# Quantised MLP of a small transformer stack: steps beside the roundings moved to GpSimd, scale chains in two parts, end tiles by halves

## The reference

```
def act_qdq(x):                                   # 16 bits, one scale for the whole tensor
    scale = max(max(abs(x)) / 32767, 1e-12)
    return clip(round(x / scale), -32768, 32767) * scale
def fixed_qdq_u16(x):
    return clip(round(x * 65536), 0, 65535) / 65536
x    = act_qdq(layernorm(x))
up   = act_qdq(x @ Wup.T)                         # Wup, Wgate, Wdown rounded to 4 bits in blocks of 32
gate = act_qdq(x @ Wgate.T)
sig  = fixed_qdq_u16(sigmoid(gate))
gate = act_qdq(gate * sig)
o    = act_qdq(gate * up)
out  = x0 + o @ Wdown.T
```

## Time and profile before

| what | value |
|---|---|
| time, median of 3 runs | 1922.03 us (1918.44 to 1930.69) |
| the profiled execution's own time | 1920.83 us |
| its span in the profile | 1919.0 us |
| mean granted TensorE clock | 0.96 of full speed |
| busy: TensorE, VectorE, ScalarE, GpSimd | 92%, 75%, 61%, 19% of the span |
| the quantised MLP in the profile | from about 1792 us to the end |

### The profile page before, as it was taken

One profiled execution on the slowest core, in us unless ns is written; L12 is line 12 of the kernel. 1 busy time (PEld: TensorE's weight loads), 2 busy tenths in 40 slices (PEclk: granted clock), 3 DMA queues, 4 the chain that ended last, 5 costly groups with the idle time before them and its releaser, 6 DMA issues. The chain is left out here.

```text
span 1919.0 us, 32646 instructions
## 1 busy us (share of the span) xinstructions
PE 1757.6 (92%) x12516; PEld 1206.2 (63%) x12516; DVE 1447.0 (75%) x1661; ACT 1173.2 (61%) x2107; POOL 369.9 (19%) x244
## 2 busy tenths in 40 slices
PE   6988989989999997999988899999999999999855
PEld 5877877457757775878776455555555555555524
DVE  6546643577899884565664799999999999997575
ACT  0333332577777764353531588888888888887373
POOL 4133120144445532232312000010010000000000
PEclk8999999999999998999989899999999999999887
DMA  9698780248866861122226855656666465540000
GB/s 358 256 350 326 273 301 1 93 161 294 319 236 243 312 237 46 68 72 69 72 36 112 170 94 123 120 100 111 118 114 115 95 120 107 104 73 8 1 0 22
DMA packets 171814, 279.78 MB, mean 146 GB/s; under 512 B 21854, under 2 KB 100478, under 8 KB 164494
## 3 DMA queue, kind: packets, MB, share of 16 engines
q1 hardware_dynamic: 170366, 277.52, 51.5%
q10 hardware_dynamic: 1296, 0.19, 0.1%
HBM read 187.07 MB, written 88.14 MB: 143 GB/s over the span
## 5 line engine op out<-in xcount | busy, mean ns | idle before, releaser
L2406 DVE TENSOR_REDUCE xn_peaks<-psum 128x2 f32<-128x1024 f32 x512 | 621.9, 1224 | 46.6 <-PE psum L2204 38.5
L2361 ACT ACTIVATE moe_mix_transposed<-psum 128x512 f32<-128x512 f32 x1024 | 552.9, 597 | 71.2 <-PE psum L2209 38.4
L2209 PE MATMUL psum<-xn_q_stack,xn_k_words 50*128 50x256 f32 x2048 | 377.3, 306 | 12.5 <-ACT y_normed L2331 5.6
L2209 PEld LDWEIGHTS psum<-xn_q_stack,xn_k_words 50*128 50x128 f32 x2048 | 249.7, 186 | 213.2 <-ACT moe_mix_transposed L2361 184.9
L2204 PE MATMUL psum<-xn_k_words,xn_q_stack 50*128 50x512 f32 x1024 | 373.3, 452 | 6.0 <-DMA xn_q_stack<-q_rows 3.8
L2241 PE MATMUL psum<-moe_mix_transposed,xn_v 128*32 128x256 f32 x4096 | 328.5, 392 | 1.9 <-issue 0.3
L2204 PEld LDWEIGHTS psum<-xn_k_words,xn_q_stack 50*128 50x128 f32 x1024 | 185.7, 185 | 14.2 <-DVE xn_peaks L2406 7.8
L934 POOL TENSOR_TENSOR mx_state<-mx_du,mx_b_all_channels 128x1024 f32<-128x1024 f32 x64 | 154.3, 2411 | 194.4 <-ACT mx_b_all_channels L1116 82.7
L1197 DVE TENSOR_TENSOR_SCAN mx_state<-psum,mx_state 128x1024 f32<-128x1024 f32 x64 | 146.2, 2285 | 49.4 <-ACT psum L1126 41.8
L324 PE MATMUL psum<-xw_ctx_natural,xw_weights_transposed 128*128 128x256 f32 x512 | 125.9, 392 | 13.5 <-DVE xw_weights_transposed L476 13.2
L2241 PEld LDWEIGHTS psum<-moe_mix_transposed,xn_v 128*32 128x32 f32 x4096 | 81.8, 108 | 74.4 <-issue 8.3
(11 more groups left out here) (351 smaller groups left out, 2549.6 us busy)
## 6 DMA issues: line engine op xcount, KB each, us to landing
xn_k_words<-k_words SPq DMA_DIRECT2D x384, 128.0 KB, 6.6
ctx_words<-xw_ctx_transposed_words SPq DMA_DIRECT2D x64, 512.0 KB
ctx_chunk_words<-ctx_words SPq DMA_DIRECT2D x64, 512.0 KB, 5.4
k_words<-ctx_k_words SPq DMA_DIRECT2D x128, 256.0 KB, 2.5
v_all<-ctx_v SPq DMA_DIRECT2D x32, 544.0 KB, 3.2
xn_v<-v_all SPq DMA_DIRECT2D x32, 544.0 KB, 4.8
xw_mask<-in_mask_BxSxS_ik SPq DMA_DIRECT2D x8, 2048.0 KB, 7.9
xw_ctx_natural<-in_ctx SPq DMA_DIRECT2D x32, 512.0 KB, 6.8
```

Of the source, the lines that this page charges most:

```text
L2209: return pe.matmul(PS[:, narrow_bank("exp", n, step, a), half * S:(half + 1) * S], K[n % XN_KSLOTS][narrow_rows(a), kt * P:(kt + 1) * P], ...
L2361: act.activation(t["weights"][:, step % 4, a, :, :], bank.rearrange("p (t s) -> p t s", t=2), ACT.Exp, scale=XN_SCALE).then_inc(s.taken, 1)
L2406: dve.tensor_reduce(t["peaks"][:, m % 2, q, :, c], PS[:, 2 * (x % 2):2 * (x % 2) + 2, :], AX.X, ALU.max).then_inc(s.top_read, 1)
```

## The change

GpSimd gets a function of its own, `mlp_pool`. It takes three kinds of steps: the subtraction of the rounding constant from the gate tiles 1 to 5 and from all up tiles (before: VectorE), the scaling and adding of the constant for the sigmoid (before: ScalarE), and the subtraction and clipping of the sigmoid (before: VectorE). In the first loop its order is gate tile m + 1, then the two sigmoid steps of tile m; VectorE keeps gate tile 0.

`scale_of` is cut in two: `spread_of` has the steps up to the diagonal, `scale_of` those behind the matmul. For scale 2 the first part now stands ahead of the last gate-times-sigmoid product and the second part right behind it.

End tiles go by halves: the gate projection of tile 0 waits for the first half of the rounded y only; the peak of the last gate tile is taken in two halves; tile 0 of the last product is rounded on VectorE, both steps, in two halves of 512 tokens, and the down projections of the first four token tiles wait for the first half only.

```diff
 def mlp_pe
     def projected(call, m, wT, made):
         for half in range(ML_HALVES):
+            if call == 0:
+                pe.wait_ge(s.q_y, KD * (half + 1))
...
-        pe.wait_ge(s.q_y, 2 * KD)
...
-        pe.wait_ge(s.q_out, m + 1)
+        pe.wait_ge(s.q_out, m + 2 if m else i * ML_HALVES // NT + 1)
...
 def mlp_act
         act.activation(t["sig"][:, m, :], t["gate"][:, m, :], ACT.Sigmoid, scale=t["scales"][:, 1, 0:1]).then_inc(s.sg, 1)
-        act.wait_ge(s.sg, m + 1)
-        act.activation(t["sig"][:, m, :], t["sig"][:, m, :], ACT.Identity, bias=k.round[:, 0:1],
-                       scale=ML_U_STEPS).then_inc(s.sr, 1)
...
-    for m in range(ML_IT):
+    for m in range(1, ML_IT):
         rounded(t["gate"][:, m, :], t["gate"][:, m, :], 4, s.r_out)
...
+def mlp_pool(k, t, s):
+    pool = k.pool
+    def gate_whole(m):
+        pool.wait_ge(s.r_gate, m + 1)
+        pool.tensor_scalar(t["gate"][:, m, :], t["gate"][:, m, :], FFN_ROUND, None, ALU.subtract).then_inc(s.q_gate, 1)
+    def sigmoid_steps(m):
+        sig = t["sig"][:, m, :]
+        pool.wait_ge(s.sg, m + 1)
+        pool.tensor_scalar(sig, sig, ML_U_STEPS, FFN_ROUND, ALU.mult, ALU.add).then_inc(s.sr, 1)
+        pool.wait_ge(s.sr, m + 1)
+        pool.tensor_scalar(sig, sig, FFN_ROUND, ML_U_STEPS - 1.0, ALU.subtract, ALU.min).then_inc(s.sq, 1)
+    pool.wait_ge(s.q_gate, 1)
+    gate_whole(1)
+    sigmoid_steps(0)
+    for m in range(1, ML_IT):
+        if m + 1 < ML_IT:
+            gate_whole(m + 1)
+        sigmoid_steps(m)
     for m in range(ML_IT):
+        pool.wait_ge(s.r_up, m + 1)
+        pool.tensor_scalar(t["up"][:, m, :], t["up"][:, m, :], FFN_ROUND, None, ALU.subtract).then_inc(s.q_up, 1)
...
 def mlp_dve
+    for half in range(ML_HALVES):
+        dve.wait_ge(s.gate, 2 * (ML_IT - 1) + half + 1)
+        largest(1, ML_IT - 1 + half, t["gate"][:, ML_IT - 1, half * BANK:(half + 1) * BANK], s.peak_gate)
...
     for m in range(ML_IT):
-        if m == 0:
-            up_largest(0)
-        if m + 1 < ML_IT:
-            gate_whole(m + 1)
-        if m:
-            up_largest(m)
-        dve.wait_ge(s.sr, m + 1)
-        dve.tensor_scalar(t["sig"][:, m, :], t["sig"][:, m, :], FFN_ROUND, ML_U_STEPS - 1.0, ALU.subtract,
-                          ALU.min).then_inc(s.sq, 1)
+        up_largest(m)
+        if m == ML_IT - 1:
+            spread_of(2, ML_IT, s.peak_up)
+        dve.wait_ge(s.q_gate, m + 1)
         dve.wait_ge(s.sq, m + 1)
         dve.scalar_tensor_tensor(t["gate"][:, m, :], t["sig"][:, m, :], 1.0 / ML_U_STEPS, t["gate"][:, m, :], ALU.mult,
                                  ALU.mult).then_inc(s.gated, 1)
+        if m == ML_IT - 1:
+            scale_of(2)
         dve.wait_ge(s.gated, m + 1)
         largest(3, m, t["gate"][:, m, :], s.peak_act)
-    scale_of(2, ML_IT, s.peak_up)
+    spread_of(3, ML_IT, s.peak_act)
     dve.wait_ge(s.unit, 2)
-    scale_of(3, ML_IT, s.peak_act, gated)
+    scale_of(3, gated)
...
     for m in range(ML_IT):
-        whole(t["up"][:, m, :], s.r_up, m, s.q_up)
         dve.wait_ge(s.r_act, m + 1)
         dve.wait_ge(s.q_up, m + 1)
...
+    spread_of(4, ML_IT, s.peak_out)
+    scale_of(4, product)
+    dve.wait_ge(s.scale, 5)
+    for half in range(ML_HALVES):
+        v = t["gate"][:, 0, half * BANK:(half + 1) * BANK]
+        dve.tensor_scalar(v, v, scales[:, 4, 1:2], FFN_ROUND, ALU.mult, ALU.add).then_inc(s.raised, 1)
+        dve.wait_ge(s.raised, half + 1)
+        dve.tensor_scalar(v, v, FFN_ROUND, None, ALU.subtract).then_inc(s.q_out, 1)
+    for m in range(1, ML_IT):
+        whole(t["gate"][:, m, :], s.r_out, m - 1, s.q_out)
```

More of the change, by code:

```diff
@@ L2918, in mlp_tiles @@
     return {"upT": k.ffn_upT, "gateT": k.ffn_gateT, "downT": k.ffn_downT,
-            "peak": sb("peak", [P, 5, ML_IT]), "top": sb("top", [P, 5]),
+            "peak": sb("peak", [P, 5, ML_IT + 1]), "top": sb("top", [P, 5]),
             "diagonal": sb("diagonal", [P, P]), "most": sb("most", [P, 5]), "unit": sb("unit", [P, 3, 2]),
@@ L2928, in mlp_sems @@
                         "most_pe most step inverse scale unit r_y q_y r_gate q_gate r_up q_up r_act r_out q_out sg sr sq gated "
-                        "product out x")
+                        "product raised out x")
 def mlp_pe(k, t, s):
@@ L3043, in mlp_act @@
         rounded(t["gate"][:, m, :], t["gate"][:, m, :], 3, s.r_act)
+    for m in range(1, ML_IT):
+        rounded(t["gate"][:, m, :], t["gate"][:, m, :], 4, s.r_out)
+def mlp_pool(k, t, s):
[16 more added lines that the diff above has]
+        sigmoid_steps(m)
     for m in range(ML_IT):
-        rounded(t["gate"][:, m, :], t["gate"][:, m, :], 4, s.r_out)
+        pool.wait_ge(s.r_up, m + 1)
+        pool.tensor_scalar(t["up"][:, m, :], t["up"][:, m, :], FFN_ROUND, None, ALU.subtract).then_inc(s.q_up, 1)
 def mlp_dve(k, t, s):
@@ L3053, in largest, with spread_of @@
         dve.tensor_reduce(peak[:, n, m:m + 1], v, AX.X, ALU.max, apply_absolute_value=True).then_inc(there, 1)
-    def scale_of(n, parts, there, of=None):
+    def spread_of(n, parts, there):
         dve.wait_ge(there, parts)
@@ L3062, in scale_of @@
         dve.tensor_scalar(t["diagonal"][:], k.ident[:], t["top"][:, n:n + 1], None, ALU.mult).then_inc(s.diagonal, 1)
+    def scale_of(n, of=None):
         dve.wait_ge(s.most_pe, n + 1)
@@ L3088, in whole @@
         dve.tensor_scalar(v, v, FFN_ROUND, None, ALU.subtract).then_inc(there, 1)
-    def gate_whole(m):
-        whole(t["gate"][:, m, :], s.r_gate, m, s.q_gate)
     def up_largest(m):
@@ L3100, in mlp_dve @@
         largest(0, g, k.Y[:, 4 * g:4 * (g + 1), :].rearrange("p t d -> p (t d)"), s.peak_y)
-    scale_of(0, KD, s.peak_y)
+    spread_of(0, KD, s.peak_y)
+    scale_of(0)
     for g in range(NT // 4):
@@ L3104, in mlp_dve @@
             whole(k.YT[:, c, g * BANK:(g + 1) * BANK], s.r_y, KD * g + c, s.q_y)
-    for m in range(ML_IT):
+    for m in range(ML_IT - 1):
         dve.wait_ge(s.gate, 2 * m + 2)
         largest(1, m, t["gate"][:, m, :], s.peak_gate)
-    scale_of(1, ML_IT, s.peak_gate)
+    for half in range(ML_HALVES):
+        dve.wait_ge(s.gate, 2 * (ML_IT - 1) + half + 1)
+        largest(1, ML_IT - 1 + half, t["gate"][:, ML_IT - 1, half * BANK:(half + 1) * BANK], s.peak_gate)
+    spread_of(1, ML_IT + 1, s.peak_gate)
+    scale_of(1)
     gated = unit_of(0, 1)
-    gate_whole(0)
+    whole(t["gate"][:, 0, :], s.r_gate, 0, s.q_gate)
     for m in range(ML_IT):
-        if m == 0:
-            up_largest(0)
-        if m + 1 < ML_IT:
-            gate_whole(m + 1)
-        if m:
-            up_largest(m)
-        dve.wait_ge(s.sr, m + 1)
-        dve.tensor_scalar(t["sig"][:, m, :], t["sig"][:, m, :], FFN_ROUND, ML_U_STEPS - 1.0, ALU.subtract,
-                          ALU.min).then_inc(s.sq, 1)
+        up_largest(m)
+        if m == ML_IT - 1:
+            spread_of(2, ML_IT, s.peak_up)
+        dve.wait_ge(s.q_gate, m + 1)
         dve.wait_ge(s.sq, m + 1)
@@ L3139, in mlp_dve @@
     dve.wait_ge(s.unit, 4)
-    scale_of(4, ML_IT, s.peak_out, product)
-    for m in range(ML_IT):
-        whole(t["gate"][:, m, :], s.r_out, m, s.q_out)
+    spread_of(4, ML_IT, s.peak_out)
[8 more added lines that the diff above has]
+        whole(t["gate"][:, m, :], s.r_out, m - 1, s.q_out)
     dve.wait_ge(s.scale, 5)
@@ L3152, in quantised_mlp @@
         t, s = mlp_tiles(k, scope), mlp_sems(k)
-        for engine in (mlp_pe, mlp_act, mlp_dve):
+        for engine in (mlp_pe, mlp_act, mlp_pool, mlp_dve):
             engine(k, t, s)
```

## The result

| | before | changed |
|---|---|---|
| median of the runs | 1922.03 us (7 runs, 1918.44 to 1936.03) | 1941.94 us (7 runs, 1927.18 to 1945.09) |
| ratio to before, 95% interval | | 1.0079 (1.0053 to 1.0106), 10 to 20 us slower |
| profiled execution | 1920.83 us, span 1919.0 | 1942.2 us, span 1940.4 |
| last block: start of the last variance step to the end of the span | 126.4 us | 138.8 us |

The kernel got slower, as forecast, but by less: 1942 us instead of 1953, and by the ratio's 0.8%, some 15 us, instead of the 31 forecast. (The ratio is the recorded estimate over all runs; the quotient of the two medians is 1.0104.)

The account below looks back on a forecast made before the run. VectorE's queue was taken as the path, with GpSimd becoming every product's supplier. Loop 1 +26.4 (start gain inside), scales +1.6, loop 2 +3.8, end -1.1 gave +30.7 us: 1953 us, 1.6% slower, range 1914 to 1966.

Parts of the forecast that it names:

- start to scale 1: Gate projections: TensorE may begin after two of four rounded pieces of y instead of four, gaining 1.3 us.
- loop 1: Loop over gate, sigmoid and up: GpSimd's queue of 17 steps delays the last product; cost 26.4 us, start gain inside.
- last product to scale 3: Scales 2 and 3: chain 3's diagonal meets GpSimd's first up step and waits to 4.8 us; cost 1.6 us.
- loop 2: Product loop: five GpSimd steps with four waits make it 23.5 us instead of 19.7; cost 3.8 us.
- end: Before the down projections: VectorE rounds half a tile in both steps, so TensorE starts earlier; gain 1.1 us.
- the exclusion of 1.0 us a turn: Both loops: VectorE products and GpSimd steps exclude each other; GpSimd waits about 1.0 us behind each product, bounds 0 and 1.23.
- T = 2.9 us: Estimated time of every moved GpSimd tensor_scalar on 128x1024 f32, extrapolated from smaller rows; bounds 2.4 and 3.3 us.
- steps under 2 us and two-operation steps far from one-operation ones: GpSimd step times in the new profile that the prediction said would make it wrong.
- The mechanism: Loop over gate, sigmoid and up: GpSimd, with 17 steps in one queue, 3 a turn, becomes the supplier of every product.
- The line-rate rival: GpSimd runs the moved steps at the cast's slope, 1.3 us each: -6 us, 1916 us; chance 0.18.
- the one without exclusion: GpSimd steps take 2.9 us but overlap VectorE's products: +18.7 us, 1941 us; chance 0.08.
- the forecast's likeliest band: Whole kernel at 1941 to 1962 us, from GpSimd steps between 2.4 and 3.3 us with exclusion; chance 0.62.

## Why the prediction was half right

Placed against the trace, from marks that both kernels have (variance step, first gate rounding, last L3122 product or L3146, first rounding by scale 3, last peak, end of the span):

| stretch | forecast | measured |
|---|---|---|
| start to scale 1 | -1.3 us | 39.7 to 38.0: -1.7 |
| scale 1 to the last product's start (loop 1) | +27.7 | 29.0 to 46.2: +17.2 |
| last product to scale 3 | +1.6 | 6.7 to 6.2: -0.5 |
| loop 2 | +3.8 | 19.7 to 19.2: -0.5 |
| end | -1.1 | 31.3 to 29.3: -2.1 |
| sum | +30.7 | +12.4 |

The forecast of 31 us failed in two of its terms: the exclusion of 1.0 us a turn, which in the changed kernel cost GpSimd's queue 0.84 us once in all, and the one price T = 2.9 us for three forms, which measured 2.77, 1.05 and 3.63. The prediction had itself named steps under 2 us and two-operation steps far from one-operation ones as signs of its being wrong, and both came.

*The mechanism* was right: GpSimd's queue of 17 steps became the supplier of every product, VectorE idle ahead of the first five, released by GpSimd, and three such steps a turn outlast the 4.84 us that VectorE had needed. Undoing one of them took 15.4 us off. The line-rate rival is refuted for the one-operation steps and for subtract-and-clip, and true for multiply-and-add. By the rule of the Trainium skill's GPSIMD Engine Reference, section 3.1 (1.03 cycles an element for up to two operations), all three steps would take, as an estimate from that figure, about what the copy takes; one of them does (1.05 us), on the other two the trace disagrees.

*One GpSimd step, T = 2.9 us*: right for the form it was drawn from (2.77). The failure is that one T was put on three forms. The 17 steps took 5 x 2.77 + 6 x 1.05 + 6 x 3.63 = 41.9 us, not 49.3: 7.4 us, of which uncounted hand-overs of some 0.05 us a step took 0.7 back. I had seen that no row showed a two-operation step on GpSimd, and had allowed them to be dearer; that one pair could be cheap and the other dear was not considered, though their mean, 2.34, made them cheaper than T.

*Who holds whom, 1.0 us a turn in both loops*: the step that failed outright. Of the 5.0 us in loop 1 0.84 came (the last clipping step, 4.47 instead of 3.63). The rows it came from the earlier trace rows show a two-input operation of 2.4 us on GpSimd, which holds its partner to its end. In the row that spoke against, at 1744 us, the GpSimd step was a tensor_scalar, the kind that the change adds, and I set the row aside for the short operand of VectorE's operation. It was the better guide, though no run shows whether an operation with such an operand is held at all.

*Scales*: the diagonal did meet GpSimd's first up step, and was held, but for 0.85 us and not to the step's end (1.13 us against the 2.7 that the forecast implied): 1.6 of the 2.1 us that the term is off. *Loop 2*: without waits GpSimd's turn is 2.74 us, close to VectorE's 2.5; the four waits that did not come are 4 of 4.3 us of the difference. *Start and end* went the right way, and by nearly the right amount once the clock is taken out: TensorE began the gates 1.1 us earlier after the variance step (forecast 1.3) and the down projections 1.0 us earlier after the last peak (forecast 1.1). The prediction had the clock at 0.50 ahead of the down projections, which held, but took their 23.8 us as fixed; they took 22.8.

In the forecast's own terms: T was too high by 0.43 us on average of 17 steps (7.4 us, and 0.8 in loop 2), the exclusion by 4 us in each loop and 1.6 at the diagonal. Both errors made the forecast too slow; with the 1.7 us that the clock gave they come to 19.7 us, of which hand-overs and small terms took 1.4 back: the 18.3 us between the two sums.

Of the rivals the one without exclusion, at 1941 us and a chance of 0.08, came nearest. Its scales and loop 2 (-1.2 and -0.4) are close to the measured -0.5 and -0.5; its loop 1 (+21.4, the start inside, against 15.5) fails by the same T. That the median of 1942 us meets its number, and the lower edge of the forecast's likeliest band, is luck: of the 21.4 us between the profiled executions 9.0 lie ahead of the block, where no term of the forecast is.

## What to carry to other kernels

When an engine is to take over a step, its price must be read for the exact form, operations and operand kinds, and not for the instruction's name: here the same subtraction costs 2.77 us written as one operation and 1.04 us written as multiply by one and add. Count the receiving engine's whole queue per turn (2.77 + 1.05 + 3.63) against the turn it has to fit into (4.84) before counting what the giving engine saves. And take the row of the same kind as the added work over more numerous rows of another kind, above all where it speaks against the term.

## What the hardware showed that was not expected

- GpSimd's tensor_scalar on f32 has three prices at 128x1024: multiply-and-add with constants 1.04 us, one operation 2.77, any other pair tried 3.63; 0.83, 2.49 and 3.3 ns for each element more, from 512 to 1024.
- A GpSimd tensor_scalar of 128x1024 holds VectorE only in a stretch of some 0.85 us at its start (the product of two SBUF tensors and the 0.69 us tensor_scalar) and in one of some 0.7 us at its end (that tensor_scalar, not the product). In between, VectorE runs free. Reductions were never held.
- The same 56 matmul instructions at the head of the block took 25.84 to 27.29 us in seven traces, by how long the granted clock stayed at 0.50 after TensorE's pause: 3.2 to 6.1 us. What ends that stretch sooner or later was not isolated.
